# Two score pairs set apart inside the product steps, each raw bank with a maximum of its own, and the output's first parts first

## The reference

```python
q, k, v = split(x @ W_q.T), split(x @ W_k.T), split(x @ W_v.T)        # 16 heads of 16
attn = softmax(scale * einsum('bnqd,bnkd->bnqk', q, k), axis=-1)
o = einsum('bnqk,bnkd->bnqd', attn, v) ... @ W_o.T
x = x + a_alpha * o
y = silu(n @ gate_w.T) * (n @ hidden_w.T) @ out_w.T + out_b           # n: x, normed and scaled; 1024 wide
return x + f_alpha * y
```

## Time and profile before

| what | before |
|---|---|
| median of 3 runs | 1012.45 us (1010.81 to 1016.49) |
| profiled execution: time, span | 1006.49 us, 1004.7 us |
| PE busy | 960.3 us (96%) |
| DVE busy | 729.3 us (73%) |
| ACT busy | 552.9 us (55%) |
| POOL busy | 273.4 us (27%) |
| mean granted clock of PE | 0.99 |

### The profile page before, as it was taken

The page is one execution under the profiler, slowest core; times in us unless marked ns, Lnnn a source line. Parts: engine busy times, 40 slices in busy tenths (PEclk is TensorE's granted clock), DMA queues, the critical chain, the costliest instruction groups (busy, mean ns, idle before and its releaser), DMA issues.

```text
span 1004.7 us, 18048 instructions
## 1 busy us (share of the span) xinstructions
PE 960.3 (96%) x6636; PEld 640.8 (64%) x6636; DVE 729.3 (73%) x1215; ACT 552.9 (55%) x1162; POOL 273.4 (27%) x262
## 2 busy tenths in 40 slices
PE   6999999999999998999899899989998999999998
PEld 4777777776545656656665575556656656655577
DVE  4988788998787785778477667857785777667254
ACT  5566455453766654565365546645653655465432
POOL 1365523222101321132222312221322222133142
PEclk9999999999999999999999999999999999999899
DMA  9635566434421130223034012302130230210000
GB/s 284 169 97 146 130 148 133 117 96 89 131 71 64 55 70 2 86 69 54 12 100 97 2 59 80 70 2 85 59 65 12 101 74 3 83 35 8 1 27 22
DMA packets 93751, 75.60 MB, mean 75 GB/s; under 512 B 44880, under 2 KB 79768, under 8 KB 93664
## 3 DMA queue, kind: packets, MB, share of 16 engines
q1 hardware_dynamic: 81880, 61.91, 23.0%
q10 hardware_dynamic: 11784, 12.54, 4.9%
HBM read 27.73 MB, written 12.61 MB: 40 GB/s over the span
## 4 chain that ended last, share of the span: by engine, by line
PE 77%; DVE 11%; ACT 4%; issue 2%; POOL 2%; SPq 2%; DMA 1%; ACTq 0%; DVEq 0%; POOLq 0%
PE bank L423 14%; PE bank L1081 11%; PE bank L1322 10%; PE bank L1062 8%; PE bank L1403 7%; PE raw_pair L979 5%; PE bank L881 4%; DVE rowmax L1012 3%; PE bank L1332 3%; PE bank L940 2%; PE bank L1144 2%; PE bank L1348 2%; PE bank L333 2%; DVE amax L486 1%; PE bank L1391 1%
## 5 line engine op out<-in xcount | busy, mean ns | idle before, releaser
L1070 ACT ACTIVATE probs<-bank 128x512 f32<-128x512 f32 x512 | 278.8, 598 | 246.6 <-PE bank L1062 246.0
L1012 DVE TENSOR_REDUCE rowmax<-raw_pair 128x2 f32<-128x1024 f32 x225 | 275.0, 1222 | 109.9 <-PE raw_pair L979 109.0
L423 PE MATMUL bank<-up_w,xs_part 128*128 128x512 f32 x768 | 192.0, 404 | 3.8 <-POOL xs_part L405 3.8
L1062 PE MATMUL bank<-q_stack,k_stack 50*128 50x512 f32 x480 | 175.2, 420 | 5.5 <-DMA q_stack<-shift_rows 3.9
L423 PEld LDWEIGHTS bank<-up_w,xs_part 128*128 128x128 f32 x768 | 143.1, 191 | 37.4 <-POOL xs_part L405 4.5
L1378 POOL TENSOR_TENSOR hid<-scratch,hid 128x512 fp32r<-128x512 f32 x64 | 81.8, 1279 | 232.1 <-ACT hid L1374 232.1
L979 PE MATMUL raw_pair<-k_stack,q_stack 48*128 48x512 f32 x440 | 136.1, 445 | 1.5 <-DVE rowmax L1012 1.5
L1081 PE MATMUL bank<-probs,v_ext 128*17 128x512 f32 x1024 | 135.7, 602 | 0.6
L1062 PEld LDWEIGHTS bank<-q_stack,k_stack 50*128 50x128 f32 x480 | 82.6, 187 | 45.2 <-ACT probs L1070 25.0
L1403 PEld LDWEIGHTS bank<-out_w,hid 64*128 64x128 f32 x1152 | 84.0, 191 | 37.8 <-issue 34.8
L1403 PE MATMUL bank<-out_w,hid 64*128 64x256 f32 x1152 | 90.1, 286 | 14.3 <-POOL hid L1378 14.2
(11 more groups left out here) (210 smaller groups left out, 1659.1 us busy)
## 6 DMA issues: line engine op xcount, KB each, us to landing
q_stack<-split SPq DMA_DIRECT2D x48, 128.0 KB, 2.9
q_stack<-hid SPq DMA_DIRECT2D x42, 128.0 KB, 2.9
k_stack<-hid SPq DMA_DIRECT2D x42, 128.0 KB, 2.9
xk<-xT SPq DMA_DIRECT2D x32, 128.0 KB, 3.0
xt<-x_tok SPq DMA_DIRECT2D x32, 128.0 KB, 2.7
x_spill<-x1t ACTq DMA_DIRECT2D x32, 128.0 KB, 2.5
xa_spill<-xa ACTq DMA_DIRECT2D x32, 128.0 KB, 2.4
x_in<-xa_spill SPq DMA_DIRECT2D x8, 512.0 KB, 5.2
```

The lines of the kernel that those rows point to most:

```text
L423: last = nc.tensor.matmul(bank[j][:], xs_part[a][:, m % 2, k, :], up_w[w][:, k, col + j * W:col + (j + 1) * W], start=(i == 0), stop=(i == ...
L1012: nc.vector.reduce_max(rowmax[:, e:e + RAWS + 1:RAWS], raw_pair[:], AX.X).then_inc(raw_read, 1)
L1062: nc.tensor.matmul(score_bank[c % 2][:], k_rows[rows, slot, kt * P:(kt + 1) * P], q_rows[rows, slot, :], start=True, stop=True).then_inc(s ...
L1070: nc.scalar.activation(probs[:, (kt % 2) * J + j, :], score_bank[c % 2][:], ACT.Exp).then_inc(exp_done, 1)
```

## The change

1. `OUT_PIECES`: the output's four parts with half 0 come first (half-steps 24 to 27), then the four with half 1 (28 to 31). Before, half 1 began at half-step 26. Since the two tiles of one bank now accumulate in between each other, only the first matmul into a bank carries `start`.
2. PE, half-steps 8 to 31 (8 to 23 in batch 7): only score 0 and raw half 1 stand at the start. Score 1, raw half 0 and in even half-steps the values are written in the middle of the six steps, after three.
3. In all batches each raw bank gets a maximum of its own (`maximum_half_dve`, L1008 in the new file), and raw half 1 waits for the maximum of bank 1 alone, raw half 0 for that of bank 0.
4. DVE, half-steps 8 to 31: the order is now maximum of bank 1, then the gate's or the product's instruction, then the maximum of bank 0 and, where due, the shift. Before, the product's instruction stood ahead of the maximum, and the maximum and the shift ahead of the gate's.

```diff
-        def maximum_halves_dve(dve, b, g, e, n):
...
+        def maximum_half_dve(dve, b, g, e, half, n):
+
+            if half == 1:
+                dve.wait_ge(raw_one_full, n + 1)
+            else:
+                dve.wait_ge(raw_full, b * (RAWS * G) + (RAWS * g + e + 1))
+            nc.vector.reduce_max(rowmax[:, e + RAWS * half:e + RAWS * half + 1], raw_pair[:, half, :], AX.X) \
+                .then_inc(raw_one_read if half == 1 else raw_read, 1)
...
-                                    start=(rows == LOWER and i == 0), stop=(rows == UPPER and i == len(PARTS) * NH - 1))
+                                    start=(rows == LOWER and i == 0 and t % HALF == 0),
+                                    stop=(rows == UPPER and i == len(PARTS) * NH - 1), skip_group_check=True)
...
-        def beside_pe(lower, upper):
-
-            for _ in range(6):
+        def beside_pe(lower, upper, middle=None):
+
+            for n in range(6):
+                if n == 3 and middle is not None:
+                    middle()
...
-        OUT_PIECES = ((0, 0), (2, 0), (0, 1), (2, 1), (1, 0), (3, 0), (1, 1), (3, 1))
+        OUT_PIECES = ((0, 0), (2, 0), (1, 0), (3, 0), (0, 1), (2, 1), (1, 1), (3, 1))
...
-            for x in range(2):
+            for x in pairs:
                 score_pe(pe, b, g, kt, 2 * (h % 2) + x)
-                if raws and ffn:
-                    raw_pe(pe, rb, rg, e, 1 - x)
-                elif raws:
-                    raw_half_pe(pe, rb, rg, e, 1 - x, h)
+                if raws:
+                    raw_half_pe(pe, rb, rg, e, 1 - x, raw_number(b, h, ffn))
...
+                parted = ffn and h >= FFN_AT and (following or h < OUT_AT)
+                excursion_pe(pe, b, h, ffn, (0,) if parted else (0, 1))
...
-                    elif p[0] == "hidden":
-                        product_dve(dve, b - 1, p[1], u + at["hidden"])
...
+                    maximum_half_dve(dve, rb, rg, e, 1, raw_number(b, h, ffn))
+                if raws and not (ffn and FFN_AT <= h):
+                    maximum_half_dve(dve, rb, rg, e, 0, raw_number(b, h, ffn))
...
+                    elif p[0] == "hidden":
+                        product_dve(dve, b - 1, p[1], u + at["hidden"])
+                if raws and ffn and FFN_AT <= h:
+                    maximum_half_dve(dve, rb, rg, e, 0, raw_number(b, h, ffn))
                     if e == RAWS - 1:
                         shift_dve(dve, rb, rg)
```

37 lines of the change are left out of this document (21 added, 16 removed).

## The result

The changed kernel takes 959.8 us (median of 4 runs, 956.14 to 960.88); the kernel before, on the same chip, 1013.63 us (4 runs). The ratio is 0.9462 (95% interval 0.9424 to 0.9501). A second series on another occasion gave 959.09 us and 0.9492 (0.9458 to 0.9526). So it is faster, and inside the range, but by 52 to 54 us where 35 were forecast. Its profiled execution took 960.88 us with a span of 959.1.

The account below looks back on a forecast made before the run. PE was taken as the bound (77% of the chain), waiting for DVE's maximum and POOL's `hid`. 20.5 + 12.7 + 2.8 - 2.6 + 2 = 35.4 us less gave 971.1, scaled by 0.6% to 977; range 957 to 993.

Parts of the forecast that it names:

- score pairs: PE's even half-steps: raw scores no longer wait for DVE's maximum; 27.7 us saved, 7.2 lost, net 20.5 us less.
- output's order: Half-step 26's wait for POOL's `hid` goes, 14.2 us; half-step 28 waits some 0.3 us, five times: 12.7 us less.
- the clock of batches 1 and 2: Without half-step 26's wait, PE's clock no longer falls behind it in these two batches: 2.8 us less.
- DVE's order: Half-steps 19, 20, 22 delayed, 7.8 us more; half-step 21 freed by gate ahead of shift, 5.2 less: 2.6 us more.
- batch 7, its waits for the shift: Half-steps 13 and 21: shifts might get free of POOL, shortening scores' DMA waits; 2 us less, bounds 0 and 6.
- main account: The forecast together with R3: a gain of 22 to 50 us, chance 0.74.
- R2: Rival: upper rows' lag hidden, DVE catches up after half-step 18, batch 7's shifts free; some 54 us gain, 958 us; chance 0.08.
- lag of the upper rows: Even half-steps: upper passes run 0.09 us late with one pair as cover, some 80 times, costing 7.2 us.
- Two maxima: On DVE, 0.68 us each against 1.22 for both banks: 31 us more work over 225 times, covered by PE.
- R1: Rival: PE waits for DVE, 0.2 to 0.3 us in some 80 pairs; gain 8 to 22, about 995 us; chance 0.12.
- R4: Rival, slower: DVE late in odd half-steps sets PE's pace, 1 us a pair and more; 1020 us and above; chance 0.03.
- R3: Rival: scores wait for the shift's DMAs, up to 1 us a batch, 6 us, 983 us; chance 0.74 together with forecast.

Follow-up runs that it names:

- x7_late_division: The changed kernel with one more reciprocal (0.25 us, result unused) ahead of the division in half-step 17 of batches 1 to 7: 962.63 us, 0.9548 of before.
- x6_gate_last: The changed kernel with DVE's gate instruction again behind both maxima and the shift in even half-steps: 960.18 us, 0.9525 of before.
- x2_own_maxima: The kernel before with only a maximum and a wait for each raw bank, all else in the old order: 998.21 us, 0.9862 of before.
- x3_old_out_order: The changed kernel with the output's old order of parts and the `start` flag belonging to it: 997.84 us, 0.9873 of before.
- x5_product_first: The changed kernel with DVE's product instruction ahead of bank 1's maximum again in odd half-steps: 956.18 us, 0.9492 of before.
- x4_one_maximum: The changed kernel with one maximum over both raw banks in batches 1 to 7, pairs still three steps apart: 1029.16 us, 1.0182 of before.

## Why the prediction was right or wrong

The spans of the two profiled executions differ by 45.6 us. Put against the terms of the sum:

| term | forecast, us less | in the traces, us less |
|---|---|---|
| score pairs | 20.5 | 18.6 |
| output's order, with the clock of batches 1 and 2 | 12.7 + 2.8 | 17.6 |
| DVE's order (the term's half-steps, 17 to 22) | -7.8 + 5.2 | 6.2 |
| batch 7, its waits for the shift | 2 | 7.4 |
| first stage | 0 | -4.3 |
| sum | 35.4 | 45.5 |

The forecast was 977 us in a range of 957 to 993, and 959.8 lies in it, but not by its main account: that gave a gain of 22 to 50 us, and the medians show 54. The range holds the result because it took in a part of R2. What the traces show is nearer, and the mechanisms can be judged one by one.

The second number column is worked out from the half-steps: output's order is half-steps 26 and 27 of batches 1 to 5 (4.6, 4.5 and three times 3.0 us) less the 0.1 of batch 6 for each; DVE's order is 0.83 us of half-step 21 and 0.2 of 20, six times; batch 7's is half-steps 15, 16 and 22 to 25; the pairs are what is left of batches 1 to 7. The rows name half-steps, not causes: as told below, most of the third row comes from the shift that is free of POOL.

- **Score pairs: right.** The even half-step was worked out at 3.04 + 0.09 = 3.13 us and takes 3.12; the lag of the upper rows, read from a single half-step of batch 7, is in every plain pair looked at. The 2 us that lack are the output's half-steps, where a pair in the middle gains 0.05 in the even ones and costs 0.11 in each odd one.
- **Two maxima: right in the sum, too large in the price.** Nothing of the added work came onto the path. It was put at 31 us from durations, 2 x 0.68 against 1.22. But an instruction on DVE that waits for nothing starts before the one ahead has ended: 0.60 us behind a 512-column maximum (537.89 and 538.49 in the changed kernel), 1.14 behind a 1024-column one. Before, batch 3:

```profile
539.22 1.23 DVE L1012 TENSOR_REDUCE rowmax<-raw_pair 128x2 f32<-128x1024 f32 x1 [0.86 <-PE raw_pair L979]
540.36 0.68 DVE L1360 SCALAR_TENSOR_TENSOR scratch<-scratch,bank 128x512 f32<-128x512 f32 x1
```

  In a row two cost 1.20 for 1.14. In half-steps 13 to 16 of batch 3, with four wide maxima replaced, DVE is busy 8.36 us and not 7.92, 0.11 each, which over 213 of them would be 23 us. The busy total is up by 3.8 only because DVE was also held up less: its shift's first two instructions went from 20.6 to 11.2 us and its division from 20.8 to 13.6.
- **DVE's order: the step that failed.** The 7.8 us for half-steps 19, 20 and 22 did not occur. I had put DVE's division behind POOL's product, where it stood before the change (1.32 us long, 0.24 behind), and it starts 0.09 us ahead of it. x7_late_division shows what the step would have cost had it been so: 0.8 us a batch, not 1.3 (and the prediction's own three pieces add up to 1.4). The 0.86 us of half-step 21 went as worked out, but for another reason than the one given. Gate ahead of shift gives 0.2 of it (x6_gate_last); 0.63 come since the shift is free of POOL, which the two maxima alone bring about (x2_own_maxima). So 5 of the row's 6.2 us aren't the order's.
- **Output's order: right.** `hid` was put at 5.3 to 5.5 us after half-step 26's start. In the changed kernel that starts at 555.39, and on POOL the product of f = 7 follows the preparation of the next input:

```profile
557.11 2.39 POOL L598 TENSOR_TENSOR xf_part<-x_in,xf_part 128x1024 fp32r<-128x1024 f32 x1 [4.68 <-ACT xf_part L584]
559.45 1.30 POOL L1380 TENSOR_TENSOR hid<-scratch,hid 128x512 fp32r<-128x512 f32 x1
...
560.64 0.39 PE L1064 MATMUL bank<-q_stack,k_stack 50*128 50x512 f32 x1
...
560.90 0.97 PE L1407 MATMUL bank<-out_w,hid 64*128 64x256 f32 x12
```

  It is done at 560.75, 5.36 us after half-step 26's start. Half-step 28's first step was due at 560.87, since half-steps 26 and 27 last 5.25 us and not the 4.99 that I had put in. So the wait of 0.3 us is none. It is hidden by 0.1 us, no more.
- **The clock: right in its place, too small in its size.** After the change the granted clock is 1.00 over half-steps 26 to 29 in batches 1 and 2 (windows of the changed kernel, columns as in the earlier trace rows):

```profile
384.60:395.20 10.60, 10.60 (x133) 7.49 (x129) 6.87 (x14) 6.11 (x11) 3.63 (x2) 1.00 0.01 2
470.00:480.60 10.60, 10.60 (x133) 7.52 (x130) 6.90 (x14) 6.16 (x11) 3.64 (x2) 1.00 0.01 2
```

  But I took one execution for all. Among the 23 runs of the kernel before in the experiments' series, those with a mean granted clock of 0.990 or 0.991 took 1004 to 1008 us, those at 0.985 to 0.988 1008 to 1012, and those at 0.979 to 0.983 1012 to 1017. The one profiled is among the first (0.990, 1006.49 us). The changed kernel's runs have 0.994 to 0.998. In most runs the waits thus seem to cost the clock more often than in the trace that I read, and this would be most of the 8 us between the 45.6 of the traces and the 54 of the medians; of the runs behind 1013.63 us themselves no clock is on record. Scaling by 0.6% was then wrong: it left in the forecast 6 us that the change largely takes away. The Trainium skill (TensorE: Matmul & The Clock Gate, "Why this matters for your kernels") warns of gaps of about 3 us; here a wait of 2.85 us was followed by the lower level in two batches of five, those of x2_own_maxima (3.02 us in batch 3) and of x3_old_out_order (4.94 us) in five of five, one of 1.88 us as well, and in batch 7 of the kernel before even one of 1.76 us. So a gap well below that figure is no safe one here.
- **Batch 7: mis-sized, 7.4 for 2.** That the shift might get free of POOL was seen, with 0.2 us for the distance, and it does, at both half-steps, 13 and 21. I kept near to none since I took the cause to be the product's later place on DVE; x5_product_first shows that this moves nothing, and that it is the exponential of score 1. And I took too little for the clock. In the trace of before it is at its lower level behind both waits:

```profile
912.50:915.80 3.30, 3.30 (x19) 2.03 (x14) 1.98 (x3) 0.39 (x1) 0.00 (x0) 0.50 0.00 0
936.40:943.10 6.70, 6.70 (x27) 4.47 (x20) 2.00 (x4) 2.37 (x5) 0.94 (x1) 0.50 0.00 0
```

  Half the clock over 10 us costs 5 us, and the two waits went from 1.76 and 2.10 to 0.72 and 0.68 us: together about the 7.4. So two thirds of this term are the clock.

Of the rivals, **R2** came nearest: more than forecast, through two of its three mechanisms (DVE not late, and batch 7's shifts free); the third, the lag hidden, did not occur. **R1** and **R4** need a DVE that works longer than PE on a pair; it is busy 8.36 of 10.00 us over the two pairs named above, and x4_one_maximum is what it looks like when the maximum does set PE's pace: 0.9 us in each even half-step. **R3** is absent from batches 1 to 6: the list has no wait for `shift_rows` outside batch 7. (Its 9.8 us from half-step 12 to 16 should have been 10.0 by the prediction's own 3.13 + 1.86, and 10.0 is what the trace has.)

## What to carry to other kernels

Where a wait comes from one engine reading two banks in one instruction, split the reading first: that gave 13 us alone and some 15 with the output's order mended. Moving the second use back in the user's order gave 14 more on top and lost without the split. The wait that remains elsewhere (the output's) must go in the same step, or it grows by as much as the others shrink. Before pricing a short DVE instruction that reads SBUF, write down its start and that of POOL's next instruction: when they are less than 0.25 us apart, both outcomes belong in the forecast, and both are to be had by moving whatever POOL waits for. And if a profiled execution has a granted clock above the other runs', count the clock's cost from the runs, not from the trace.

## What the runs showed of the hardware

- **A start order decides over 1.1 us.** DVE's division took 0.42 us when it started 0.09 us ahead of POOL's product and 1.51 to 1.55 when it started 0.02 to 0.05 us behind. The shift's instructions took 0.17 or 0.18 us or 1.17 to 1.24 in the same way. When DVE was first, POOL's instruction took 1.48 in place of 1.29. This is the rule of the Trainium skill (SBUF — State Buffer, "Who interferes with whom"), and the traces agree: the one that starts first holds up the other. New to me was what hangs on it: 0.8 us a batch for one, 8 us of batch 7 for the other.
- **Durations on DVE overstate what a split costs.** A 512-column maximum lasts 0.68 us, a 1024-column one 1.22, but the next instruction starts 0.60 and 1.14 us behind: 1.20 for 1.14 in a row, and 0.11 us of busy time for each split in the changed kernel's order.
- **A wait of 1.76 us was followed by the lower clock level** (batch 7 of the kernel before, 0.50 over the next 3.3 us), and so was one of 1.88 (batch 6 of x3_old_out_order), while one of 2.85 us in the kernel before was not the earlier trace rows, nor one of 1.80 us in batch 7 of x2_own_maxima (granted clock 1.00 from 904.5 to 915.0). The length of the wait alone doesn't tell; what else decides stays open. None of PE's waits of 0.6 to 1 us in batches 1 to 7 was followed by it, in any kernel here. A fall lasted 3.4, 6.8 or 10.2 us and so cost 1.7, 3.4 or 5.1.
